# Second attention of a four-layer decoder: queries read by SP between the value writes, masks in two steps, and another order of work on four engines

## What is computed

```python
q = (query @ Wq + bq).reshape(B, Sq, nh, hd).transpose(0, 2, 1, 3)
k = (key @ Wk + bk).reshape(B, Sk, nh, hd).transpose(0, 2, 1, 3)
v = (value @ Wv + bv).reshape(B, Sk, nh, hd).transpose(0, 2, 1, 3)
scores = jnp.einsum('bhqd,bhkd->bhqk', q, k)
ids = _relative_ids(Sq, Sk, MAX_REL)
rel_k = rel_key_table[ids]
scores = scores + jnp.einsum('bhqd,qkd->bhqk', q, rel_k)
attn = jax.nn.softmax(scores / jnp.sqrt(jnp.asarray(hd, scores.dtype)), axis=-1)
out = jnp.einsum('bhqk,bhkd->bhqd', attn, v)
out = out + jnp.einsum('bhqk,qkd->bhqd', attn, rel_value_table[ids])
return out.transpose(0, 2, 1, 3).reshape(B, Sq, H) @ Wo + bo
```

## Time and profile before

| what | value |
|---|---|
| median of three runs | 2211.84 us (2209.42 to 2215.06) |
| the profiled execution's own time | 2210.14 us |
| its span, first to last instruction | 2208.4 us |
| granted TensorE clock, mean of the span | 0.97 |
| second attention, first projections to last statistics | about 1205 to 1809 us |
| busy in the span: PE, DVE, ACT, POOL | 93%, 87%, 70%, 71% |

### The profile page before, as it was taken

The page is one execution under the profiler, slowest core; times in us unless marked ns, Lnnn a source line. Parts: engine busy times, 40 slices in busy tenths (PEclk is TensorE's granted clock), DMA queues, the critical chain, the costliest instruction groups (busy, mean ns, idle before and its releaser), DMA issues. The chain is left out here.

```text
span 2208.4 us, 82850 instructions
## 1 busy us (share of the span) xinstructions
PE 2051.3 (93%) x28378; PEld 1570.9 (71%) x28380; DVE 1913.1 (87%) x4327; ACT 1554.9 (70%) x3516; POOL 1575.4 (71%) x1457
## 2 busy tenths in 40 slices
PE   3999999977999999999996899999999966999999
PEld 2788888854666666666664889999999953666666
DVE  5899999987888888888887789999999868888888
ACT  3788888865555555555554677777777756888887
POOL 1567777643666666666665889999999943888887
PEclk9999999988999999999998899999999978999999
DMA  5000000004322222222221445555555520000000
GB/s 155 12 6 6 6 6 6 7 1 90 93 90 80 81 87 80 81 88 78 83 79 26 78 78 86 80 80 85 82 80 80 84 67 1 15 9 14 9 14 15
DMA packets 476443, 121.41 MB, mean 55 GB/s; under 512 B 431879, under 2 KB 446855, under 8 KB 475604
## 3 DMA queue, kind: packets, MB, share of 16 engines
q1 hardware_dynamic: 343988, 86.86, 18.2%
q10 hardware_dynamic: 132384, 33.63, 6.7%
HBM read 106.51 MB, written 13.89 MB: 55 GB/s over the span
## 5 line engine op out<-in xcount | busy, mean ns | idle before, releaser
L1220 POOL TENSOR_TENSOR f_low<-f_hidden,f_high 128x512 f16<-128x512 f32 x336 | 442.6, 1323 | 217.0 <-ACT f_high L1152 215.1
L1178 DVE TENSOR_TENSOR f_hidden<-f_hidden,f_share 128x512 f32<-128x512 f32 x336 | 374.1, 1114 | 0.0
L1367 POOL TENSOR_TENSOR f_low<-f_hidden,f_high 128x512 f16<-128x512 f32 x256 | 297.1, 1161 | 74.5 <-ACT f_high L1310 74.1
L1158 ACT ACTIVATE f_act_out<-f_gate 128x512 f32<-128x512 f32 x336 | 200.4, 597 | 192.4 <-PE f_gate L1122 192.4
L1201 DVE SCALAR_TENSOR_TENSOR f_hidden<-f_up,f_act_out 128x512 f32<-128x512 f32 x336 | 229.7, 684 | 83.6 <-PE f_up L1122 50.6
L1152 ACT ACTIVATE f_high<-f_hidden 128x512 f16<-128x512 f32 x336 | 210.5, 626 | 73.0 <-DVE f_hidden L1178 71.7
L1132 PE MATMUL f_y<-w_high,f_high 128*128 128x128 f16 x1344 | 242.4, 219 | 2.2 <-POOL f_low L1220 2.2
L1132 PE MATMUL f_y<-w_high,f_low 128*128 128x128 f16 x1344 | 242.4, 219 | 0.0
L1132 PE MATMUL f_y<-w_low,f_high 128*128 128x128 f16 x1344 | 242.4, 219 | 0.0
L1768 POOL TENSOR_TENSOR a_q_head_high<-a_q_t_high,a_head_mask 128x2048 f16<-128x2048 f16 x64 | 232.9, 3639 | 8.0 <-DVE a_q_t_low L1845 8.0
L1768 POOL TENSOR_TENSOR a_q_head_low<-a_q_t_low,a_head_mask 128x2048 f16<-128x2048 f16 x64 | 232.9, 3639 | 0.0
(11 more groups left out here) (279 smaller groups left out, 8165.1 us busy)
## 6 DMA issues: line engine op xcount, KB each, us to landing
f_share<-expert_shares SPq DMA_DIRECT2D x128, 256.0 KB, 3.2
a_q_pos<-queries ACTq DMA_DIRECT2D x64, 512.0 KB, 4.4
f_share<-expert_shares SPq DMA_DIRECT2D x128, 128.0 KB, 3.0
relative_values<-a_rel_all SPq DMA_DIRECT2D x512, 8.0 KB, 2.5
x_all<-in_x SPq DMA_DIRECT2D x4, 1024.0 KB, 7.8
f_share<-expert_shares SPq DMA_DIRECT2D x128, 32.0 KB, 1.8
queries<-a_q_parts SPq DMA_DIRECT2D x64, 64.0 KB, 3.0
a_rel<-relative_values SPq DMA_DIRECT2D x64, 64.0 KB, 1.7
```

The costliest lines, as they stand in the source:

```text
L1158: nc.scalar.activation(act_out[m % RING][:, :], gate_ps[m % BANKS][:, :], ACT.Silu, scale=1.0 / WSCALE).then_inc(act_ready, 1)
L1178: nc.vector.tensor_tensor(hidden[r][:, :], hidden[r][:, :], share[k][:, :, :].rearrange("p t q -> p (t q)"), ALU.mult).then_inc(scaled, 1)
L1220: nc.gpsimd.tensor_tensor(low[r][:, :], hidden[r][:, :], high[r][:, :], ALU.subtract).then_inc(low_ready, 1)
L1367: nc.gpsimd.tensor_tensor(low[k][:, :], hidden[k][:, :], high[k][:, :], ALU.subtract).then_inc(low_ready, 1)
```

## The change

Nothing is computed in another way and no instruction is added or taken away; all of it is order and place.

- read_queries goes from ACT's queue to SP's, reads n+2 instead of n+1, and stands between the two halves of write_relative(n-1). write_queries goes to the end of SP's slot and writes n+3 instead of n+2.
- mask_queries is called for one part at a time: the low part of n+1, then the high part of n+2, both ahead of add_relative(n-2). POOL's slots run from FIRST to LAST.
- On PE scores(n+1,0) is now the end of slot n. fin_project opens the slot, and turns, mix_turn, project and relative stand in other places between the scores.
- On ACT copy_rows(n-1) takes the place of copy_rows(n-2) in the slot after, copy_relative(n,0) comes to the end of slot n, and the exponentials, high_parts, normalize and copy_xn stand elsewhere.
- On DVE inverse_sum(n-1) is the last of the slot instead of inverse_sum(n-2) in the next; subtract_max, statistics, residual and low_mixed are moved.

```diff
--- before.py
+++ after.py
@@ -1485,10 +1485,16 @@
                         sp.dma_start(q_written[p], q_parts[p][:, :, :].rearrange("q a (d h) -> q (a d) h", d=HD)
                                      ).then_inc(q_out[p], 16)
 
-                def write_relative(n, p):
+                def read_queries(n, p):
+                    if inside(n, 0, B):
+                        sp.wait_ge(q_out[p], (n - p) * 8 + 16)
+                        wait(sp, score_ready, 4 * n - 4)
+                        sp.dma_start(q_pos[p][:, :, :], q_read[p]).then_inc(q_in[p], 16)
+
+                def write_relative(n, p, half):
                     if inside(n, 0, B):
                         sp.wait_ge(rel_copied, 4 * n + 4)
-                        for c in range(QC):
+                        for c in range(QC // 2 * half, QC // 2 * (half + 1)):
                             sp.dma_start(r_written[p][c], rel_all[p][c:P:QC, :, HD * c:HD * (c + 1)]
                                          ).then_inc(r_out[p], 16)
 
@@ -1498,9 +1504,12 @@
                         sp.dma_start(rel[p][:, :, :].rearrange("q h d -> q (h d)"), r_dram[p]).then_inc(r_in[p], 16)
 
                 def slot(n, p):
+                    o = 1 - p
                     read_relative(n - 2, p)
-                    write_queries(n + 2, p)
-                    write_relative(n - 1, 1 - p)
+                    write_relative(n - 1, o, 0)
+                    read_queries(n + 2, p)
+                    write_relative(n - 1, o, 1)
+                    write_queries(n + 3, o)
 
                 slots(sp, FIRST, LO, HI, LAST, slot)
 
@@ -1617,24 +1626,24 @@
 
                 def slot(n, p):
                     o = 1 - p
-                    scores(n, p, 0)
+                    fin_project(n - 4, p)
                     scores(n, p, 1)
+                    relative(n - 1, o, 0)
                     turn(n - 1, 2)
-                    fin_project(n - 4, p)
-                    relative(n - 1, o, 0)
+                    mix_turn(n - 2)
                     turn(n - 1, 3)
+                    relative(n - 1, o, 1)
                     project(n, p)
-                    mix_turn(n - 2)
-                    relative(n - 1, o, 1)
                     scores(n, p, 2)
+                    turn(n, 0)
+                    relative(n - 1, o, 2)
                     scores(n, p, 3)
                     fin_turn(n - 3, o)
-                    relative(n - 1, o, 2)
-                    turn(n, 0)
                     turn(n, 1)
                     mix(n - 1, o)
+                    relative(n - 1, o, 3)
                     prep_turn(n + 3, o)
-                    relative(n - 1, o, 3)
+                    scores(n + 1, o, 0)
 
                 pe.wait_ge(weights_ready, 2)
 
@@ -1650,12 +1659,6 @@
                 act.wait_ge(weights_in, 16 * len(WEIGHTS))
                 act.wait_ge(weights_ready, 1)
                 nc.scalar.activation(w_out[0][:, :], w_o[:, :], ACT.Copy).then_inc(w_out_high, 1)
-
-                def read_queries(n, p):
-                    if inside(n, 0, B):
-                        act.wait_ge(q_out[p], (n - p) * 8 + 16)
-                        wait(act, score_ready, 4 * n - 4)
-                        act.dma_start(q_pos[p][:, :, :], q_read[p]).then_inc(q_in[p], 16)
 
                 def copy_xn(n, p):
                     if inside(n, 0, B):
@@ -1730,24 +1733,23 @@
 
                 def slot(n, p):
                     o = 1 - p
-                    read_queries(n + 1, o)
-                    copy_rows(n - 2)
                     high_prob(n - 1, o, 2)
-                    copy_relative(n - 1, o, 0)
+                    exp(n, 0)
                     high_prob(n - 1, o, 3)
+                    copy_relative(n - 1, o, 1)
+                    exp(n, 1)
                     high_parts(n, p)
-                    copy_relative(n - 1, o, 1)
-                    exp(n, 0)
-                    exp(n, 1)
                     copy_relative(n - 1, o, 2)
                     high_prob(n, p, 0)
-                    normalize(n + 4, p)
                     high_mixed(n - 3, o)
                     exp(n, 2)
                     high_prob(n, p, 1)
                     copy_relative(n - 1, o, 3)
+                    copy_rows(n - 1)
+                    exp(n, 3)
+                    normalize(n + 4, p)
                     copy_xn(n + 3, o)
-                    exp(n, 3)
+                    copy_relative(n, p, 0)
 
                 slots(act, FIRST, LO, HI, LAST, slot)
 
@@ -1760,15 +1762,14 @@
                 last.then_inc(cleared, 1)
                 pool.wait_ge(weights_ready, 3)
 
-                def mask_queries(n, p):
+                def mask_queries(n, p, k):
                     if inside(n, 0, B):
                         pool.wait_ge(proj_low, n + 1)
                         wait(pool, score_ready, 4 * n - 4)
-                        for k in range(2):
-                            nc.gpsimd.tensor_tensor(q_head[p][k][:, :, :],
-                                                    q_t[p][k][:, :].unsqueeze(2).broadcast_to([P, P, NH]),
-                                                    head_mask[:, :].unsqueeze(1).broadcast_to([P, P, NH]),
-                                                    ALU.mult).then_inc(q_head_ready, 1)
+                        nc.gpsimd.tensor_tensor(q_head[p][k][:, :, :],
+                                                q_t[p][k][:, :].unsqueeze(2).broadcast_to([P, P, NH]),
+                                                head_mask[:, :].unsqueeze(1).broadcast_to([P, P, NH]),
+                                                ALU.mult).then_inc(q_head_ready, 1)
 
                 def add_relative(n, p):
                     if inside(n, 0, B):
@@ -1788,10 +1789,11 @@
                 def slot(n, p):
                     o = 1 - p
                     divide(n - 3, o)
-                    mask_queries(n + 1, o)
+                    mask_queries(n + 1, o, 1)
+                    mask_queries(n + 2, p, 0)
                     add_relative(n - 2, p)
 
-                slots(pool, -1, LO, HI, B + 3, slot)
+                slots(pool, FIRST, LO, HI, LAST, slot)
 
             @block.vector
             def _(dve):
@@ -1910,25 +1912,25 @@
 
                 def slot(n, p):
                     o = 1 - p
+                    low_prob(n - 1, o, 2)
                     subtract_max(n, 1)
-                    low_prob(n - 1, o, 2)
+                    statistics(n - 4)
+                    low_prob(n - 1, o, 3)
                     sum_parts(n - 2, p)
-                    inverse_sum(n - 2, p)
-                    low_prob(n - 1, o, 3)
                     row_max(n, 2)
                     low_parts(n, p)
                     subtract_max(n, 2)
                     row_max(n, 3)
+                    low_mixed(n - 3, o)
                     subtract_max(n, 3)
                     low_prob(n, p, 0)
-                    low_mixed(n - 3, o)
                     low_prob(n, p, 1)
+                    residual(n - 3)
                     low_xn(n + 3, o)
                     row_max(n + 1, 0)
+                    subtract_max(n + 1, 0)
                     row_max(n + 1, 1)
-                    residual(n - 3)
-                    subtract_max(n + 1, 0)
-                    statistics(n - 4)
+                    inverse_sum(n - 1, o)
 
                 slots(dve, FIRST, LO, HI, LAST, slot)
```

## The result

| | before | after |
|---|---|---|
| median, us (four runs of each, side by side) | 2212.32 | 2188.93 |
| lowest to highest | 2209.42 to 2215.06 | 2186.11 to 2193.54 |
| profiled execution, its span | 2210.14, 2208.4 | 2186.11, 2184.2 |
| ratio of the times | | 0.9896, 95% interval 0.9874 to 0.9919 |

A forecast was written before the change was run, and what follows sets the result against it. The prediction took POOL, held in a loop through SP, to pace the slot. Steady slots -15.3 and early slots -3 gave -18.3, from 2211.84 to 2193.5 us; range 2185 to 2211.

The forecast's parts named there:

- the early slots recover too: Rival: the eight slots before the 51 steady ones come to 8.6 us, -8 more, near 2188; chance 0.15.
- So the slot is paced by POOL: Before scores(n,0) PE waits 0.52 us for POOL's low mask; a loop through SP of about 17.7 us per two slots.
- The floor of 8.49: PE's blocks for one slot, read as gap-free, last 8.49 us; against a period of 8.83 PE loses 0.34.
- Masks in two steps, cost 0: On POOL one mask of 3.64 us instead of two stands between add and scores; loop falls to 14.1 us, cost 0.
- Order on PE, ACT and DVE, cost 0: The new order costs 0 on these engines, and ACT's 88.4 us of waiting in front of copy_rows go.
- ACT's copy_relative waits for a_rel: Sign of being wrong: ACT waiting for a_rel at copy_relative, which the walk had arriving in time.
- SP's round of 8.2 us: SP's queue: 5.56 us issuing, 2.2 tail and 0.45 make 8.2, below the slot's 8.5 by 0.3.
- writes that start in the moment of the read back: Sign of being wrong on SP: writes starting as the read back is issued mean SP's round is the bound.
- The sum: 51 steady slots at 8.53 instead of 8.83 give -15.3, early slots -3, preparation and last slots 0: total -18.3 us.
- The branch: The loop's branch, turning every two slots, was given 0.04 us a slot above 8.49, at most 0.12.
- One queue: Rival at SP's wait for the eighth write's landing: tail 3.3, round 9.3 us, +24, about 2236; chance 0.13.
- The wait only changes its name: Rival, no change: ACT waits for a_rel, SP's round is 8.8, or the branch causes PE's loss; 2208 to 2213; chance 0.12.

The follow-up runs named there:

- Run 1: The kernel before with only POOL's order changed (low mask of n+1, high mask of n+2, then the add): ratio 1.0005, median 2218.00 us.
- Run 4: The kernel before with only the order of PE, ACT and DVE changed, masks and transfers as before: ratio 0.9990, median 2215.67 us.
- run 3: The kernel before with masks and transfers changed, the order of PE, ACT and DVE as before: ratio 0.9900, median 2196.27 us.
- run 5: The changed kernel with the transfers as before, so masks and order only: ratio 0.9940 to the kernel before, median 2205.68 us.
- run 9: The changed kernel again with no edit, on another chip: ratio 0.9895 to the kernel before, median 2189.50 us.
- run 10: The changed kernel with the query read, of n+1, issued by ACT behind high_prob(n-1,2): ratio 0.9836 to the kernel before, median 2176.52 us.
- run 6: The changed kernel with POOL as before, both masks of n+1 ahead of the add: ratio 1.0074 to the kernel before, median 2236.27 us.
- run 7: The changed kernel with ACT's wait for a_rel at copy_relative(n,0) made by SP ahead of its writes: ratio 0.9905 to the kernel before, 2198.99 us.
- run 11: The changed kernel with the query read early on ACT and the wait for a_rel on SP: ratio 0.9830 to the kernel before, 2174.76 us.

## Why the prediction came out right, and where it was wrong

The forecast was 2193.5, -18.3; measured were 2188.93, -23.4. The direction held, and so did the mechanism of the masks, as far as it went. That the result lies near the 2188 of the rival "the early slots recover too" is chance: the early slots did not recover, and the steady ones gave more. By its own steps:

**"So the slot is paced by POOL" was half of it.** The loop it named is real: relative 3, copy, eight writes, read back, add, both masks, scores, about 17.7 us for two slots. A second one of the same length ran beside it, which the prediction saw only as ACT's 88.4 us: the eight writes, their landing, the query write behind them on SP, its landing, the query read at the head of ACT's queue, and ACT's work to the next copy_relative 3. Its stations in the kernel before, from eight writes to those two slots later:

```profile
1603.90 5.10 SPq L1492 DMA_DIRECT2D relative_values<-a_rel_all  x8
1610.80 0.37 SPq L1485 DMA_DIRECT2D queries<-a_q_parts  x1
1613.93 0.39 ACTq L1658 DMA_DIRECT2D a_q_pos<-queries  x1
1620.91 0.38 ACT L1715 ACTIVATE a_rel_all<-a_rel 128x256 f32<-128x256 f32 x1
1621.32 5.25 SPq L1492 DMA_DIRECT2D relative_values<-a_rel_all  x8
```
That is 17.42 us, in which ACT waits 0.56 for PE. Run 1 opens the first loop alone and gains nothing (1.0005). Run 4 opens the second alone and gains nothing (0.9990), but it lengthens the first as well, so it says less of the second's worth. Runs 3 and 5 open both and gain 1.0% and 0.6%. The prediction made both edits in one walk, so the sum came out right with one loop missing; of masks alone it would have been wrong.

**The floor of 8.49 was too high.** It was called gap-free, and it held a wait. In the earlier trace rows mix_turn with relative takes 0.92 (1659.43 to 1660.35), 0.57 before relative's 0.35. The kernel after does mix_turn in 0.43:

```profile
1604.26 0.60 PE L1605 MATMUL a_mix<-ident,a_mixed_rows 128*128 128x128 f32 x4
1604.69 0.60 PE L1568 MATMUL a_trans<-a_by_head_ident,a_prob 128*77 128x128 f32 x4
1605.23 0.19 PE L1579 MATMUL a_rel<-table_high,a_prob_t_high 77*128 77x64 f16 x1
...
1605.57 0.20 PE L1526 MATMUL a_prep<-ctx_t_high,table_high 128*128 x1
```
The kernel before, in another slot, on ACT and on PE:

```profile
1570.42 0.60 ACT L1722 ACTIVATE a_mixed_rows<-a_rows 128x512 f32<-128x512 f32 x1 [1.59 <-DMA queries<-a_q_parts]
...
1571.40 0.38 ACT L1715 ACTIVATE a_rel_all<-a_rel 128x256 f32<-128x256 f32 x1
```

```profile
1571.08 0.66 PE L1596 MATMUL a_mix<-ident,a_mixed_rows 128*128 128x128 f32 x4
1571.92 0.19 PE L1570 MATMUL a_rel<-table_high,a_prob_t_high 77*128 77x64 f16 x1 [0.19 <-ACT a_rel_all L1715]
```
Here mix_turn takes 0.84, and the row of relative names the wait. In the slot of the earlier trace rows the wait was 0.14, shorter than the modelled tail of the matmuls ahead of it, so no row showed an idle PE. Slots without any gap last 8.30 to 8.31 in runs 9 and 10, and 8.325 is the steady period of run 10. PE therefore lost 8.83 - 8.30 = 0.53 a slot before, not 0.34. The gap before scores(n,0) was not all of it either. Between 1330 and 1740 us the kernel before takes 0.63 on average from relative 3 to these scores, where 0.35 is gap-free (the slot of the earlier trace rows took 0.87), and 0.61 for mix_turn, where 0.44 is: 0.28 and 0.17 lost.

**Masks in two steps, cost 0: right.** POOL waits 10.1 us for a_rel in all, and run 6 shows what the unsplit masks cost.

**Order on PE, ACT and DVE, cost 0: right, and its gain beside the other two parts is not measurable** (run 3 against the result and run 9: 0.9900, 0.9896, 0.9895). That copy_rows loses its wait was right. ACT's copy_relative waits for a_rel, which the prediction named as a sign of being wrong; runs 7 and 11 gain nothing by taking that wait away.

**SP's round of 8.2 us, 0.3 below the slot: mis-sized by 0.25, as the balance of two larger errors.** The terms were 5.56 of issuing, 2.2 of tail and 0.45. The 49 rounds of the kernel after have a mean of 8.43: 6.59 from the first write to the end of the last, 1.35 from there to the read back, 0.48 to the next write. So the issuing was 1.0 longer than said and the tail 0.85 shorter; that 8.2 came so near was luck. The 1.0 lies in the first write behind the query read, 1.38 us instead of 0.61, and in small steps between the instructions. The round of the rows above, 8.28 from the first write to the read back, is a long one; the mean is 7.94, and 7.61 in run 10, where the issuing takes 5.1 again and the tail 2.47. The 2.2 was taken from a round called steady that lies ahead of the 51 steady slots; these had 1.55 in the kernel before. The sign the prediction had given for being wrong, writes that start in the moment of the read back, is there. It had compared 8.2 with a floor of 8.49; against the true 8.30 nothing was spare.

The Trainium skill (DMA: Bandwidth & Descriptors, "Issuing engines are not separate DMA queues") says that issuing from several engines saves only sequencer time. Run 10 agrees: with the read issued by ACT the share of the DMA engines is the same 0.55, and what SP saves is issue time. Here that saving is worth 13 us, since SP's sequencer is full. From the rule of ring order in the Trainium skill (the same page, "Queues, rings and completion order") the prediction feared a longer tail of the writes behind the read; what grew was the issue of the first of them, and the tail fell to 1.35.

**The sum.** Steady slots -19.8 for -15.3 predicted: the floor is 0.19 lower than said, and SP's round takes 0.14 of that back, where 0.04 had been set aside for the branch. Early slots -4.6 for -3, within its bounds of 0 and -8.6. The first add came 1.9 later, where 0 was said. **The branch** of 0.04 a slot was not needed: in runs 1 and 3, where scores(n,0) opens PE's slot, the step from relative 3 to scores is 0.35 and some 0.57 in turn, 0.22 every second slot; in the order of the changed kernel no such gap shows. That it is the branch is argued from its place and its turn. PE's slots in run 3 are 8.36 and some 8.58 in turn, a mean of 8.47 against the 8.30 of the new order. So the order does lower PE's floor, and that this gains nothing beside run 3 fits SP's round of 8.4 to 8.5 in both; no run has the query read on ACT without the new order, which would show it.

**The rivals.** "One queue" had the right bound, SP's round, by the wrong term: it wanted a tail of 3.3 and a round of 9.3, and got a tail of 1.35, a slower issue and a round of about 8.44, 0.14 above the floor. "The wait only changes its name" and "the early slots recover too" did not come: the early slots take 9.03, not 8.6.

What stays open: why the first issue behind the read is slow, and why the kernel before differs by 0.3% between chips.

## What to carry to other kernels

When two resources wait on each other in a ring through several engines, list every ring and its length before pricing an edit; with two rings of one length an edit to one alone can be worth nothing, and both together the whole. Measure a floor between starts of blocks in several slots and take the shortest of each block, since a wait shorter than the modelled tail of a matmul shows as busy. A sequencer that only issues transfers is an engine with a period of its own: sum its issue times and its wait for landings, and put nothing more on it when that sum is within a few per cent of the slot.

## What the runs showed of the hardware

Issue times depend on what was issued to the same queue. A write of 8 KB takes 0.61 us on SP (5.11 for eight) as long as the 512 KB read is issued by ACT, as in run 10 at the same total traffic (DMA share 0.55 in both windows). With the read in SP's own queue the first write behind it takes 1.38 us on average (1.05 to 1.79 in 49 rounds) and the three behind that 0.61 again. In the six other runs with the read there the first takes 1.40 to 1.56 on average. The 64 KB query write takes 0.53 instead of 0.37. The tail goes the other way: from the end of the writes to the read back it is 1.35 us with the read in SP's queue and 2.47 in run 10 (1.55 in the kernel before, whose ACT issues the read 1.47 us behind the first write on average, for 2.43 in run 10). The landing of the read back went from 1.7 us to 2.1, in run 10 to 1.9, so not all of that is the queue:

```profile
a_rel<-relative_values SPq DMA_DIRECT2D x64, 64.0 KB, 2.1
```
The kernel before had medians of 2212.32, 2217.48, 2219.90 and 2212.51 us on the chips it was timed on, 0.3% apart, while the ratios of the changed kernel to the kernel beside it are 0.9896 and 0.9895. The ratios can be compared between chips, the times can't.
